# Router logits as extra columns, idle products before the gathered rows, and three roots in one batch, in a vision tower with routed experts

## The chip, the cores and the metric

One core of a Trainium2 chip runs the kernel. The metric is the device time of one execution in microseconds, as the median of three runs. The engines are TensorE (PE, its weight loads PEld), VectorE (DVE), ScalarE (ACT), GpSimd (POOL) and SyncE (SP, which issues most transfers). Each works through its own instructions in order and waits on semaphores. TensorE's clock has two levels here, 1.2 and 2.4 GHz; the profile gives the granted clock as a share of the upper one.

## What is computed

Cut to what matters:

```python
# x: 64 images of 3 x 96 x 96, 36 patches of 768 values, 256 channels, 8 experts
z = layernorm(layernorm(patches, ln1) @ W_proj + b_proj, ln2)      # 64 x 36 x 256
h = concat(cls, z) + pos_emb                                       # 37 tokens an image
x1 = norm(h)                                                       # no gain, no offset
q, k, v = x1 @ Wq.T + bq, x1 @ Wk.T + bk, x1 @ Wv.T + bv
h = h + softmax(masked(q @ k.T / 256)) @ v                         # a token does not see itself
x2 = norm(h)
logits = x2 @ router_w + router_b                                  # 8 experts
gates, experts = top2(softmax(logits))                             # gates sum to 1
# per expert the 444 tokens with the highest gates are kept
out_e = (gelu(x2[tok] @ w1[e] + b1[e]) @ w2[e] + b2[e]) * gate     # 256 -> 1024 -> 256
out = h + layernorm(scatter_add(out_e), ln)
```

The norm without gain divides by sqrt(var + 1e-5).

## The kernel before

The 2368 tokens are cut into 22 tiles of three images, 111 rows padded to 112. Behind a head of loads the kernel runs a software pipeline over the tiles: each engine has a function `step(i, slot)`, called for i = 0 to 27 in order, of which a middle part is a hardware loop over four steps at a time (ACT and DVE 6 to 17, POOL 7 to 18, PE 9 to 20). In `step(i)` an engine works for several tiles at once, each at another stage: the order of the blocks `t = i - k` in the source is the order of the queue. In the loop the waits go against register values, and `plain` adds a semaphore increment behind them.

Followed by one tile t, the stages are these. DVE takes the statistics of the patches (`stats_x`, L1046), POOL makes their root (`scale_x`), ACT normalises (L562), TensorE transposes in step t-1 (`turn_x`, L759), ACT and DVE split the result into a high and a low part (L568, L1055). TensorE multiplies by W_proj in step t (18 products, L829) and adds the bias (L831). DVE takes the statistics of z (L1129, L1137: zstat, zmv) and z2 (L1148); POOL makes the root (`rstd` with zmv); ACT scales into the residual tile H (L619); POOL adds the position (L1548); DVE takes the statistics of h (L1198, L1200: hmv). In step t+1 POOL makes the root and the offset of x1 (`scaled` with hmv), ACT makes x1 (L609). In step t+2 TensorE transposes x1 (L819), ahead of the 18 products of that step's z; in step t+3 it makes the product with the combined query-key matrix (L779), the values (L786) and the scores (L804), and transposes the probabilities at its end (L873); in step t+4 the product with the values (L812). DVE adds it to H (L1193, g_h). Then come the statistics gmv (L1133, L1141), their root on POOL (`scaled` with gmv), x2 on ACT (L633), its transpose on TensorE (L839, step t+5), its copy on ACT (L585), the product with `rw` (L795, step t+6) and the copy of the 8 logits into LG (L614).

`rstd` is an addition of epsilon (L1480) and a power of -0.5 (L1482), both on one column; `scaled` adds a multiplication by the negative mean (L1488). POOL does this four times a step: for h, z, g and the patches of a later tile. POOL also builds tables in steps 2 to 4 (`masks_table`, `live_table`, `index_table`).

In step 0 TensorE transposes Wq and Wk (L850), in step 1 it multiplies them (L858) and makes bias products of one column (L863, L866), which ACT copies out (L622 to L625). The column ED of `wv` and `bvb` carries a bias term of the scores with the values.

Behind the pipeline comes the routing. DVE picks the two best experts for the first 16 tiles in steps 22 and 23 and their gates in step 25 (`best`, `gates`, L1108 on), and the last 6 tiles when all 22 columns of LG are there. ACT repeats the gates (L665) for TensorE to transpose (L879), and an eight-round search finds each expert's threshold (L1228 to L1238, L892). Lists of tokens are made by products of one-hot rows: a short list for expert 0 (L904), then the full one in two halves (`lists`, L911). POOL gathers expert 0's rows of x2 by the short list (L1573); TensorE transposes them in two halves (`first_gathered`, L920), before each half of the full list. Then it runs, for each expert and each of 8 blocks of the hidden width, `hidden` (L944) and `project` (L961), with a gelu (L712), a cast (L724) and a difference (L1334) between them. DVE's queue there is written out by hand: the first differences, `read_lists`, two weight differences, then the first L1334.

## Time and profile before

| | |
|---|---|
| median of 3 runs | 421.92 us (421.41 to 422.31) |
| the profiled execution | 423.82 us |
| its span, first to last instruction | 421.4 us |
| PE, PEld busy | 349.8 us (83%), 312.1 us (74%) |
| DVE busy | 316.3 us (75%) |
| ACT busy | 259.0 us (61%) |
| POOL busy | 240.4 us (57%) |
| mean granted TensorE clock | 0.909 |

```profile
## 2 busy tenths in 40 slices
PE   2689999999999999660024999999999999999940
PEld 0478889999899997450013899999999999999930
DVE  7665878788777865868888555778787878787772
ACT  3336677778777785445700478686868686868520
POOL 4156888778778876310004433248686868654574
PEclk9989999999999999955555699999999999999995
```

A slice is 10.5 us and a digit is the busy share in tenths. PEclk is the granted clock in tenths: 9 is the upper level, 5 the lower.

### The profile page before, as it was taken

Reading aid. Unit: us, or ns where it says so; the run is one execution under the profiler, and the core shown is the slowest. Engines: PE = TensorE matmul, PEld = TensorE weight load, DVE = VectorE, ACT = ScalarE, POOL = GpSimd, SP = SyncE. Lnnn points to the kernel's source line nnn. Section 1 sums busy time; section 2 is a strip of 40 time slices with the busy share of each in tenths; the row PEclk is TensorE's granted clock in tenths of the full one; section 3 lists DMA queues with packets and bytes.
Section 4 is the critical chain, followed back from the end, with each engine's and each line's share of the span. In section 5 each row is a group of like instructions: output and inputs, shape, how many; then the busy total and the mean of one; then the engine's idle time right before and its main releaser. Section 6 shows DMA issues by size and latency. Waiting matters only on the chain. (4 is left out here: it accounts for less than half of the span.)

```text
span 421.4 us, 8094 instructions
## 1 busy us (share of the span) xinstructions
PE 349.8 (83%) x2190; PEld 312.1 (74%) x2190; DVE 316.3 (75%) x868; ACT 259.0 (61%) x548; POOL 240.4 (57%) x434
## 2 busy tenths in 40 slices
PE   2689999999999999660024999999999999999940
PEld 0478889999899997450013899999999999999930
DVE  7665878788777865868888555778787878787772
ACT  3336677778777785445700478686868686868520
POOL 4156888778778876310004433248686868654574
PEclk9989999999999999955555699999999999999995
DMA  6632043544535398658703587467777777752221
GB/s 185 194 64 64 2 109 109 148 135 125 145 117 144 100 121 150 169 164 239 5 0 87 154 213 192 149 155 209 209 213 206 213 207 212 206 177 56 65 76 54
DMA packets 49278, 58.38 MB, mean 139 GB/s; under 512 B 12167, under 2 KB 38007, under 8 KB 49244
## 3 DMA queue, kind: packets, MB, share of 16 engines
q1 hardware_dynamic: 42602, 43.11, 39.4%
q0 software_dynamic: 5568, 14.09, 12.7%
q10 hardware_dynamic: 1074, 0.79, 0.6%
q8 instruction: 14, 0.23, 0.2%
q14 instruction: 20, 0.16, 0.2%
HBM read 36.74 MB, written 21.36 MB: 138 GB/s over the span
## 5 line engine op out<-in xcount | busy, mean ns | idle before, releaser
L944 PE MATMUL pz<-halves 128*128 128x448 f32 x384 | 90.4, 372 | 0.0
L961 PE MATMUL pall<-halves 128*128 128x448 f32 x384 | 89.7, 369 | 0.8 <-DVE halves L1334 0.8
L944 PEld LDWEIGHTS pz<-halves 128*128 128x128 f32 x384 | 73.7, 192 | 6.1
L961 PEld LDWEIGHTS pall<-halves 128*128 128x128 f32 x384 | 71.1, 189 | 6.8 <-DVE halves L1334 1.1
L1573 POOL DMA_INDIRECT held<-x_rows,gidx x32 | 33.8, 1057 | 65.3 <-DVE gidx L1276 41.2
L712 ACT ACTIVATE wproj<-pz,b1t 128x448 f32<-128x448 f32 x64 | 40.7, 636 | 47.1 <-PE pz L944 41.3
L1334 DVE TENSOR_TENSOR halves<-wproj,halves 128x448 fp32r<-128x448 f32 x64 | 40.2, 628 | 30.5 <-ACT halves L724 25.0
L829 PE MATMUL pall<-halves 128*112 128x256 f32 x396 | 52.5, 287 | 4.6 <-DVE halves L1055 4.6
L1482 POOL TENSOR_TENSOR rs<-rs,neghalf 112x1 f32<-112x1 f32 x88 | 50.2, 570 | 7.3
L829 PEld LDWEIGHTS pall<-halves 128*112 128x112 f32 x396 | 48.1, 177 | 5.0 <-DVE halves L1055 2.7
L1598 POOL DMA_INDIRECT out<-rows,didx x28 | 37.2, 1330 | 25.6 <-DVE rows L1382 15.9
L724 ACT CAST halves<-wproj 128x448 fp32r<-128x448 f32 x64 | 36.3, 567 | 2.0
L1581 POOL DMA_INDIRECT rows<-sums,sidx x28 | 29.3, 1047 | 7.8 <-issue 7.5
L1307 DVE TENSOR_TENSOR halves<-stage,halves 128x512 fp32r<-128x512 f32 x32 | 22.0, 687 | 7.2 <-ACT halves L656 7.2
L562 ACT ACTIVATE stage<-stage,rs 112x768 f32<-112x768 f32 x22 | 22.4, 1019 | 5.3 <-POOL rs L1488 5.3
L1046 DVE BATCH_NORM_STATS2 xstat<-stage 112x6 f32<-112x384 f32 x44 | 22.3, 549 | 3.6 <-DMA stage<-in_x 3.6
L779 PE MATMUL pall<-x1T,wq 128*128 128x112 f32 x176 | 24.2, 281 | 0.5 <-ACT x2T L585 0.4
L568 ACT CAST halves<-pz 128x672 fp32r<-128x672 f32 x22 | 15.8, 719 | 12.6 <-PE pz L759 12.6
L786 PE MATMUL pall<-wv,x1T 128*112 128x257 f32 x88 | 22.8, 380 | 0.0
L779 PEld LDWEIGHTS pall<-x1T,wq 128*128 128x128 f32 x176 | 21.3, 191 | 1.8 <-issue 0.9
L1313 DVE TENSOR_TENSOR halves<-stage,halves 128x512 fp32r<-128x512 f32 x32 | 21.9, 683 | 0.0
L1055 DVE TENSOR_TENSOR halves<-pz,halves 128x672 fp32r<-128x672 f32 x22 | 18.8, 855 | 3.4 <-ACT halves L568 2.6
(265 smaller groups left out, 716.7 us busy)
## 6 DMA issues: line engine op xcount, KB each, us to landing
stage<-in_w SPq DMA_DIRECT2D x32, 512.0 KB, 5.0
stage<-in_x SPq DMA_DIRECT2D x64, 108.0 KB
x_rows<-x SPq DMA_DIRECT2D x22, 224.0 KB, 2.8
x_rows<-held SPq DMA_DIRECT2D x22, 224.0 KB, 4.2
sums<-rows SPq DMA_DIRECT2D x7, 448.0 KB
out<-held SPq DMA_DIRECT2D x21, 111.0 KB
x_rows<-zero SPq DMA_DIRECT2D x1, 1474.9 KB
wproj<-in_w_proj ACTq DMA_DIRECT2D x1, 768.0 KB
```

The source lines that it names most:

```text
L712: nc.scalar.activation(hr[:, k % 2, :], bank(k % 2)[:, 0:SLOTS], ACT.Gelu, bias=col(b1t, u)).then_inc(u_sb, 1)
L724: nc.scalar.copy(hh[:, k % 2, :], hr[:, k % 2, :]).then_inc(h_hi, 1)
L779: m = nc.tensor.matmul(bank(3)[:, o * P:(o + 1) * P], wqk[:, c, o * 128:(o + 1) * 128], xt_[:, c, :], start=(c == 0), stop=(c == EC - 1))
L786: m = nc.tensor.matmul(bank(4)[0:P, 0:ED + 1], xt_[:, c, :], wv[:, c, :], start=(c == 0), stop=(c == EC - 1))
L829: nc.tensor.matmul(bank(2)[0:P, 0:ED], xs[:, c * P:(c + 1) * P], w[:, c, :], start=(c == k == 0), stop=False)
L944: m = nc.tensor.matmul(bank(k % 2)[:, 0:SLOTS], w[:, c, k * 128:(k + 1) * 128], xs[:, e % 2, c, :], start=(n == 0), stop=(n == 3 * EC - 1))
L961: m = nc.tensor.matmul(pall[:, 2 * (e % 2) + o, 0:SLOTS], w[:, k, o * 128:(o + 1) * 128], hs[:, k % 2, :], start=(k == 0 and n == 0), stop ...
L1334: V_.tensor_tensor(hl[:, k % 2, :], hr[:, k % 2, :], hh[:, k % 2, :].bitcast(fp32), ALU.subtract)\
L1482: G.tensor_tensor(rs[:, slot, 1:2], rs[:, slot, 0:1], neghalf[:, :], ALU.pow).then_inc(done, 1)
L1573: pool.indirect_dma_start(xg[:, e % XB_N, j, :], None, x2_rows, bass.IndirectOffsetOnAxis(ap=gidx[:, k:k + 1], axis=0)).then_inc(g_in[e % ...
L1581: pool.indirect_dma_start(prev[:, j, :], None, sums[0:1 + e * SLOTS, :], bass.IndirectOffsetOnAxis(ap=sidx[:, k:k + 1], axis=0)).then_inc( ...
L1598: pool.indirect_dma_start(out, bass.IndirectOffsetOnAxis(ap=didx[0:n, k:k + 1], axis=0), final_of(e)[0:n, j, :], None, bounds_check=IMAGES ...
```

## The change

Three edits.

First, the logits. x2 @ rw is 1/sqrt(var_g + eps) times the centred h, after attention, times rw. With `rwc`, the router weights less their mean over the channels, the centring falls away, so the kernel carries (h @ rwc) as 8 more columns through the attention. `wv` and `bvb` get 8 columns Wv.T @ rwc (they pass through the probabilities with the values) and 8 columns rwc, whose product with x1, times `dev` = (var_h + eps)/sqrt(var_h + eps), is the residual's part; ACT writes it into the 8 columns behind each tile of H, which is now 264 wide. DVE's addition of L1193 adds both. ACT scales the 8 columns into LG. The transpose, copy and product of x2 and their semaphores are gone.

Second, the roots of z (tile i), h (tile i-1) and g (tile i-4) are made by one addition and one power over up to three neighbouring columns, behind one wait for all three statistics; `nrm` is double-buffered by step.

Third, 24 products of the identity by itself stand ahead of the first gathered rows.

```diff
-        wv = sb("wv", [128, EC, ED + 1])
+        HW = ED + E
+        VW = HW + 1 + E
+        wv = sb("wv", [128, EC, VW])
+        rwc = wv[:, :, HW + 1:VW]
@@ scalar, step @@
-                t = i - 5
-                if live(t):
-                    need(act, x2T_ps, t + 1)
-                    need(act, l_ps, t)
-                    nc.scalar.copy(x2T[:, :], bank(3)[:, 256:256 + EC * P]).then_inc(x2T_sb, 1)
@@ i == 0 @@
+                    act.wait_ge(c_vT, 1)
+                    nc.scalar.copy(wvs[:, :, :], bank(5)[:, 0:EC * ED].rearrange("p (c e) -> p c e", c=EC)).then_inc(c_ws, 1)
+                    nc.scalar.copy(bvrep[:, :, :], bank(7)[:, 0:EC * P].rearrange("p (c r) -> p c r", c=EC)).then_inc(c_ws, 1)
...
                 t = i - 4
                 if live(t):
-                    plain(act, (x2T_ps, t - 1), (x2_out[slot], 16 * (t // 4) if isinstance(t, int) else (t - slot) * 4),
+                    plain(act, (n_rs, i + 1), (g_h, t + 1))
+                    nc.scalar.activation(LG[:, :, at(t)] if not isinstance(t, int) else LG[:, :, t:t + 1],
+                                         tile_of(H, t, ED, HW).rearrange("p (e a) -> p e a", a=1), ACT.Copy,
+                                         scale=norm(par, 1, 2)).then_inc(l_sb, 1)
...
+                t = i - 2
+                if live(t):
+                    plain(act, (h_dev, t + 1), (v_sb, t + 1))
+                    nc.scalar.activation(tile_of(H, t, ED, HW), v[:, par, HW + 1:VW], ACT.Copy, scale=dev[:, odd:odd + 1])\
+                        .then_inc(h_rw, 1)
@@ tensor, step @@
-                        m = nc.tensor.matmul(bank(4)[0:P, 0:ED + 1], xt_[:, c, :], wv[:, c, :],
+                        m = nc.tensor.matmul(bank(4)[0:P, 0:VW], xt_[:, c, :], wv[:, c, :],
                                              start=(c == 0), stop=(c == EC - 1))
-                t = i - 6
-                if live(t):
-                    need(pe, x2T_sb, t + 1)
-                    need(pe, l_sb, t)
-                    need(pe, z_2, i if not isinstance(i, int) else min(i, TILES))
-                    for c in range(EC):
-                        m = nc.tensor.matmul(bank(2)[0:P, 256:256 + E], x2T[:, c * P:(c + 1) * P], rw[:, c, :],
-                                             start=(c == 0), stop=(c == EC - 1))
-                    m.then_inc(l_ps, 1)
...
-                    nc.tensor.matmul(bank(7)[0:P, 0:ED], probT[:, :], v[:, par, 0:ED], start=True, stop=True)\
+                    nc.tensor.matmul(bank(7)[0:P, 0:HW], probT[:, :], v[:, par, 0:HW], start=True, stop=True)\
...
-                        m = nc.tensor.transpose(bank(3)[:, 256 + c * P:256 + (c + 1) * P],
-                                                x2[:, (slot + 3) % 4, c * 128:(c + 1) * 128], ident[0:P, 0:P])
-                    m.then_inc(x2T_ps, 1)
@@ i == 0 @@
+                    for o in range(EC):
+                        for c in range(EC):
+                            nc.tensor.transpose(bank(5)[:, o * ED + c * 128:o * ED + (c + 1) * 128],
+                                                wv[:, c, o * 128:(o + 1) * 128], ident[:, :])
+                    for c in range(EC):
+                        nc.tensor.transpose(bank(7)[:, c * P:(c + 1) * P], bvb[:, c * 128:(c + 1) * 128], ident[0:P, 0:P])
+                    pe.wait_ge(c_idx, 2)
+                    for c in range(EC):
+                        m = nc.tensor.matmul(bank(6)[:, 0:E], onesf[:, :], rw[:, c, :], start=(c == 0), stop=(c == EC - 1))
+                    m.then_inc(c_vT, 1)
@@ i == 1 @@
+                    pe.wait_ge(c_ws, 4)
+                    pe.wait_ge(c_rw, 1)
+                    for c in range(EC):
+                        for o in range(EC):
+                            nc.tensor.matmul(bank(4)[:, 3 * EC + c * E:3 * EC + (c + 1) * E],
+                                             wvs[:, o, c * 128:(c + 1) * 128], rwc[:, o, :],
+                                             start=(o == 0), stop=(o == EC - 1))
+                    for o in range(EC):
+                        m = nc.tensor.matmul(bank(4)[0:P, 3 * EC + EC * E:3 * EC + EC * E + E], bvrep[:, o, :], rwc[:, o, :],
+                                             start=(o == 0), stop=(o == EC - 1))
@@ ahead of the first gathered rows @@
+            def keep_clock(n):
+
+                for _ in range(n):
+                    nc.tensor.matmul(bank(3)[:, 0:128], ident[:, :], ident[:, :], start=True, stop=True)
+            keep_clock(24)
             for h in range(2):
                 first_gathered(h)
                 lists(h)
@@ vector, step, i == 0 @@
+                    V_.memset(bvb[:, HW + 1:VW], 0.0)
+                    dve.wait_ge(c_vT, 1)
+                    V_.scalar_tensor_tensor(rwc, rep(bank(6)[:, 0:E].rearrange("p (a e) -> p a e", a=1), 1, EC),
+                                            -1.0 / ED, rw[:, :, :], ALU.mult, ALU.add).then_inc(c_rw, 1)
@@ gpsimd, step @@
-                t = i - 1
-                if live(t):
-                    need(pool, x1_ok, t)
-                    scaled(2, hmv, h_mv, t + 1, h_rs0, h_rs, h_nb)
-                t = i
-                if live(t):
-                    need(pool, z_sc, t)
-                    rstd(1, zmv, z_mv, t + 1, z_rs0, z_rs)
-                t = i - 4
-                if live(t):
-                    need(pool, x2_ok, t)
-                    scaled(3, gmv, g_mv, t + 1, g_rs0, g_rs, g_nb)
+                par = slot % 2
+                on = [k for k, back in enumerate((0, 1, 4)) if live(i - back)]
+                if on:
+                    a, b = on[0], on[-1] + 1
...
+                    plain(pool, *[((z_mv, i + 1), (h_mv, i), (g_mv, i - 3))[k] for k in on])
+                    G.tensor_scalar(nrm[:, par, 0, a:b], nmv[:, a:b, 1], EPS, None, ALU.add).then_inc(n_rs0, 1)
+                    need(pool, n_rs0, i + 1)
+                    G.tensor_tensor(nrm[:, par, 1, a:b], nrm[:, par, 0, a:b], rep(neghalf[:, :], 1, b - a), ALU.pow)\
+                        .then_inc(n_rs, 1)
+                    plain(pool, (n_rs, i + 1))
+                    for k, done in ((1, h_nb), (2, g_nb)):
+                        if k == 1 and k in on:
+                            G.tensor_tensor(dev[:, par:par + 1], norm(par, 0, 1), norm(par, 1, 1), ALU.mult).then_inc(h_dev, 1)
+                        if k in on:
+                            G.tensor_scalar(norm(par, 2, k), nmv[:, k, 0:1], norm(par, 1, k), -1.0, ALU.mult, ALU.mult)\
+                                .then_inc(done, 1)
```

`onesf` is set on POOL in the head in place of step 2, and ACT copies two more small results in step 1.

## Rows read from the trace of the kernel before

**Rows 1.** Timeline of one loop step, TensorE: start, duration, instruction, idle time before.

```profile
119.39 0.37 PE L831 MATMUL pall<-zbias,ones 2*112 2x256 f32 x1
119.68 0.41 PE L839 MATMUL pall<-ident,x 112*128 112x112 f32 x2
119.93 0.74 PE L759 MATMUL pz<-ident,stage 112*128 112x112 f32 x6
121.57 1.03 PE L786 MATMUL pall<-wv,x1T 128*112 128x257 f32 x4
122.44 0.47 PE L795 MATMUL pall<-rw,x2T 128*112 128x8 f32 x4
122.77 0.62 PE L804 MATMUL pall<-x1T,tT 128*112 128x112 f32 x4
123.66 0.35 PE L819 MATMUL pall<-ident,x 112*128 112x112 f32 x2
126.07 0.37 PE L831 MATMUL pall<-zbias,ones 2*112 2x256 f32 x1
```

**Rows 2.** The same step on the other engines, behind one earlier row.

```profile
42.91 0.26 POOL L1488 TENSOR_SCALAR rs<-hmv,rs 112x1 f32<-112x1 f32 x1
...
119.79 0.43 DVE L1129 BATCH_NORM_STATS2 zstat<-pall 112x6 f32<-112x256 f32 x1
120.73 0.18 DVE L1141 BATCH_NORM_AGGREGATE gmv<-gstat 112x2 f32<-112x6 f32 x1
122.10 0.27 POOL L1488 TENSOR_SCALAR rs<-hmv,rs 112x1 f32<-112x1 f32 x1 [0.21 <-POOL rs L1482]
122.44 0.22 POOL L1480 TENSOR_SCALAR rs<-zmv 112x1 f32<-112x1 f32 x1
122.47 0.60 ACT L609 ACTIVATE x<-held,rs 112x256 f32 x1
122.75 0.57 POOL L1482 TENSOR_TENSOR rs<-rs,neghalf 112x1 f32<-112x1 f32 x1
123.51 0.51 ACT L619 ACTIVATE held<-z,rs 112x256 f32 x1 [0.24 <-POOL rs L1482]
125.02 0.21 DVE L1051 BATCH_NORM_AGGREGATE xmv<-xstat 112x2 f32<-112x12 f32 x1
125.43 0.22 POOL L1480 TENSOR_SCALAR rs<-xmv 112x1 f32<-112x1 f32 x1
```

**Rows 3.** The power on POOL on two and on four columns: timeline, then line L1590.

```profile
408.77 0.73 POOL L1590 TENSOR_TENSOR frs<-frs,neghalf 112x2 f32<-112x2 f32 x1
...
L1590 POOL TENSOR_TENSOR frs<-frs,neghalf x9: 722/1045/1051, 271.4 to 414.7; 112x4 f32<-112x4 f32 x7, 112x2 f32<-112x2 f32 x2
```

**Rows 4.** Timeline of DVE: the statistics of z of tiles 2, 6 and 21.

```profile
34.22 0.43 DVE L1129 BATCH_NORM_STATS2 zstat<-pall 112x6 f32<-112x256 f32 x1 [3.20 <-PE pall L831]
...
59.71 0.43 DVE L1129 BATCH_NORM_STATS2 zstat<-pall 112x6 f32<-112x256 f32 x1
...
159.80 0.43 DVE L1129 BATCH_NORM_STATS2 zstat<-pall 112x6 f32<-112x256 f32 x1 [1.17 <-PE pall L831]
```

**Rows 5.** Timeline of TensorE in the head: the one-column products of step 1.

```profile
29.27 1.84 PE L863 MATMUL pall<-bqk,scratch 128*128 128x1 f32 x16
```

**Rows 6.** Timeline at the end of the pipeline: gates on DVE, repeated gates on ACT.

```profile
178.48 0.20 DVE L1108 TENSOR_SCALAR dl<-ed 112x16 f32<-112x16 f32 x1 [0.57 <-ACT ed L649]
...
183.25 1.90 ACT L665 COPY scratch<-V 112x2048 f32<-112x2048 f32 x1
```

**Rows 7.** TensorE's timeline before the experts; then 238 to 240 us by engine, with PEclk.

```profile
220.15 2.19 PE L904 MATMUL pall<-scratch 112*112 112x4 bf16 x22 [4.63 <-DVE scratch L1266]
...
234.13 4.83 PE L944 MATMUL pz<-halves 128*128 128x448 f32 x12
...
238.79 1.59 PE L961 MATMUL pall<-halves 128*128 128x448 f32 x6
...
238.00:240.00 2.00, 2.00 (x8) 1.50 (x7) 1.23 (x2) 1.48 (x3) 1.70 (x2) 0.74 0.94 306
```

More of the change, by code:

```diff
@@ L154, in vit_tower @@
         zstat = sb("zstat", [P, 6])
-        zmv = sb("zmv", [P, 2])
         z2 = sb("z2", [P, ED])
         hstat = sb("hstat", [P, 6])
-        hmv = sb("hmv", [P, 2])
         x1 = sb("x1", [P, 2, ED])
@@ L171, in vit_tower @@
         gstat = sb("gstat", [P, 6])
-        gmv = sb("gmv", [P, 2])
         x2 = sb("x2", [P, 4, ED])
-        x2T = sb("x2T", [128, EC * P])
-        rs = sb("rs", [P, 4, 3])
+        rs = sb("rs", [P, 1, 3])
+        nmv = sb("nmv", [P, 3, 2])
+        zmv, hmv, gmv = (nmv[:, k, :] for k in range(3))
+        nrm = sb("nrm", [P, 2, 3, 3])
+        dev = sb("dev", [P, 2])
         held = sb("held", [P, XB_N * JT * XW])
-        assert TILES * ED <= XB_N * JT * XW
-        H = held[:, 0:TILES * ED].rearrange("p (t f) -> p t f", t=TILES)
+        assert TILES * HW <= XB_N * JT * XW
+        H = held[:, 0:TILES * HW].rearrange("p (t f) -> p t f", t=TILES)
         xg = held[:, :].rearrange("p (s j f) -> p s j f", s=XB_N, j=JT)
@@ L489, in step @@
                     need(sp, hb, t + 1)
-                    tile = H[:, t:t + 1, :] if isinstance(t, int) else H[:, bass.ds(t, 1), :]
+                    tile = H[:, t:t + 1, 0:ED] if isinstance(t, int) else H[:, bass.ds(t, 1), 0:ED]
                     dram = hb_v[:, 2 * t:2 * t + 2, :] if isinstance(t, int) else hb_v[:, bass.ds(t * 2, 2), :]
@@ L608, in step @@
                     plain(act, (x1T_ps, t - 1), (h_nb, t + 1))
-                    nc.scalar.activation(x1[:, odd, :], tile_of(H, t), ACT.Identity, bias=rs[:, 2, 2:3],
-                                         scale=rs[:, 2, 1:2]).then_inc(x1_ok, 1)
-                t = i - 5
-                if live(t):
-                    plain(act, (l_ps, t + 1))
-                    nc.scalar.copy(LG[:, :, at(t)] if not isinstance(t, int) else LG[:, :, t:t + 1],
-                                   bank(2)[0:P, 256:256 + E].rearrange("p (e a) -> p e a", a=1)).then_inc(l_sb, 1)
+                    nc.scalar.activation(x1[:, odd, :], tile_of(H, t), ACT.Identity, bias=norm(par, 2, 1),
+                                         scale=norm(par, 1, 1)).then_inc(x1_ok, 1)
                 t = i
                 if live(t):
-                    plain(act, (z_2, t + 1), (z_rs, t + 1))
-                    nc.scalar.activation(tile_of(H, t), z2[:, :], ACT.Copy, scale=rs[:, 1, 1:2]).then_inc(z_sc, 1)
+                    plain(act, (z_2, t + 1), (n_rs, i + 1))
+                    nc.scalar.activation(tile_of(H, t), z2[:, :], ACT.Copy, scale=norm(par, 1, 0)).then_inc(z_sc, 1)
                 if isinstance(i, int) and i == 1:
@@ L825, in step @@
                     need(pe, z_2, t)
-                    need(pe, l_sb, t - 5)
                     for c in range(PC):
@@ L832, in step @@
                         .then_inc(z_ps, 1)
-                t = i - 5
-                if live(t):
-                    need(pe, x2_ok, t + 1)
-                    need(pe, x2T_sb, t)
-                    need(pe, t_sb, t + 3 if not isinstance(t, int) else min(t + 3, TILES))
-                    for c in range(EC):
-                        m = nc.tensor.transpose(bank(3)[:, 256 + c * P:256 + (c + 1) * P],
-                                                x2[:, (slot + 3) % 4, c * 128:(c + 1) * 128], ident[0:P, 0:P])
-                    m.then_inc(x2T_ps, 1)
                 t = i + 1
@@ L1135, in step @@
                 if live(t):
-                    plain(dve, (z_st, t + 1), (z_rs0, t))
-                    V_.bn_aggr(zmv[:, :], zstat[:, :]).then_inc(z_mv, 1)
+                    plain(dve, (z_st, t + 1), (n_rs0, t))
+                    V_.bn_aggr(zmv, zstat[:, :]).then_inc(z_mv, 1)
                 t = i - 4
@@ L1140, in step @@
                     plain(dve, (g_st, t + 1), (g_nb, t))
-                    V_.bn_aggr(gmv[:, :], gstat[:, :]).then_inc(g_mv, 1)
+                    V_.bn_aggr(gmv, gstat[:, :]).then_inc(g_mv, 1)
                 t = i
@@ L1163, in step @@
                     need(dve, o_ps, t - 1)
-                    V_.tensor_tensor(v[:, par, :], bank(4)[0:P, 0:ED + 1], bvb[:, :], ALU.add).then_inc(v_sb, 1)
+                    need(dve, h_rw, t - 1)
+                    V_.tensor_tensor(v[:, par, :], bank(4)[0:P, 0:VW], bvb[:, :], ALU.add).then_inc(v_sb, 1)
                     plain(dve, (s_ps, t + 1), (p_ok, t), (s_nmx, t))
@@ L1191, in step @@
                 if live(t):
-                    need(dve, r_inv, t + 1)
-                    V_.scalar_tensor_tensor(tile_of(H, t), bank(7)[0:P, 0:ED], rinv[:, 0:1], tile_of(H, t),
+                    plain(dve, (r_inv, t + 1), (h_rw, t + 1))
+                    V_.scalar_tensor_tensor(tile_of(H, t, 0, HW), bank(7)[0:P, 0:HW], rinv[:, 0:1], tile_of(H, t, 0, HW),
                                             ALU.mult, ALU.add).then_inc(g_h, 1)
```

80 lines of the change are left out of this document (45 added, 35 removed).

## The prediction

> **What bounds the kernel now.** I read the page first: TensorE is 83% busy and, in its slices, at nine tenths and full clock in two stretches, the token and attention loop (to about 170 us) and the experts (from about 240 us to the end), with the router's search between them at the lower clock. The change touches the loop, the search's entry and the experts' first products.
>
> In the loop I read the timeline of one step. TensorE has no idle mark in it: from one bias product L831 to the next are 6.68 us, and everything else has its answer early enough [rows 1]. The 15 steps between the statistics at 59.71 and 159.80 take 6.67 us each [rows 4]. So a TensorE product taken out saves its own time, until some other chain of one step is as long. I therefore looked for such a chain in the new program before adding up savings.
>
> **Router logits out of TensorE's stream.** Gone per step: two transposes of x2 (L839, 119.68 to 119.93: 0.25 us) and the logits products (L795, 122.44 to 122.77: 0.33 us) [rows 1]. Added: 16 columns in the value products and 8 in the residual product. L786 with 257 columns takes 0.87 us for two products (121.57 to 122.44) [rows 1], so 0.43 us for one; 16 more in each of two and 8 more in one are 0.07 us. Net 0.51 us: were TensorE still the limit, a step would be 6.16 us.
>
> **The roots as one batch: a new ring.** Before, x1's root belongs to tile i-1 and is made first on POOL; ACT starts x1 at 122.47 and TensorE wants its transpose L819 at 123.66 [rows 1, 2]. Now POOL's one addition waits for zmv of tile i too. ACT's x1 of tile i-1 thus hangs on z of tile i, and TensorE transposes that x1 ahead of z of tile i+1, in order. This is a chain that must be walked once a step:
> - L831 to zstat 0.40 (119.39 to 119.79); zstat to the end of gmv 1.12 (120.91) [rows 1, 2].
> - to POOL 0.20 (xmv ends 125.23, L1480 at 125.43); addition and gap 0.31 (122.44 to 122.75) [rows 2].
> - the power. One column takes 0.57 [rows 2], two 0.73, four 1.045 [rows 3]: 0.16 a column, so three columns 0.885, an estimate between two measured widths.
> - gap 0.21 (the mark at L1488) [rows 2]; dev, a product that the trace does not show: not below L1480's 0.22, not above the power's 0.57; it is one arithmetic step on one column, so I take 0.22; gap 0.08; the scale 0.27.
> - to ACT 0.19 (the power ends 123.32, ACT starts 123.51), x1 0.60 [rows 2]; to TensorE 0.10, an estimate: no row shows TensorE waiting for x1 here, the nearest handover is POOL's at 122.37 to ACT's start at 122.47 [rows 2].
> - L819 to L831 2.41 (123.66 to 126.07) [rows 1].
> Sum 7.00 us, against 6.67 now: TensorE idles 0.84 us a step and the step is 0.33 us longer. For the 12 steps that ACT and DVE run as a loop (6 to 17) +3.9 us. In the last three (18 to 20) the waits are constants and shorter: L1488 at 42.91, outside the loop, has no idle mark where the loop's has 0.21 [rows 2]. Four such handovers at 0.1 less make about 6.6 us: -0.3 us. Bounds of the ring: with the power at two columns' 0.73 and TensorE next at once 6.75 (+0.9 us in 12 steps); with power 1.045 and dev 0.57 7.51 (+10 us).
>
> The GPSIMD Engine Reference of the Trainium skill (Elementwise, side-by-side cycle accounting) puts the price in a per-instruction part and about 2.6 cycles per element. By that, two more columns cost nothing one could see, which is rival B. The trace disagrees for the power, at 0.16 us a column [rows 3], and the sum goes by the trace.
>
> POOL itself gets freer: two power instructions of 0.57 us and two additions less a step. That gives nothing, since POOL's tile additions wait for ACT's z. The queue behind the batch on POOL (position, x scaling, ln_b) ends about 0.8 us before the next gmv. On ACT the x2T copy goes and the small h_rw copy comes, at the step's end, where ACT then waits for TensorE; the wider DVE additions (8 and 16 columns) lie in DVE's waits; together 0, at most 0.1 us a step if they reached the ring. SP's queue is the same.
>
> **The head (steps 0 to 5).** Step 0's new transposes, the ones product, two ACT copies and rwc on DVE lie in waits that step 0 has for its tiles anyway; nothing, up to 0.5 us. Step 1's six small products (12 instructions) lie on the path, between the q-k products and z of tile 2. At L863's rate (1.84 us for 16) [rows 5] they are 1.4 us, at L795's (0.33 for four [rows 1]) 1.0; I take 1.2 us. From step 2 on the ring holds too. Now 34.22 to 59.71 is 25.49 us for four steps [rows 4]. With constant waits the ring is about 6.1 us with two live norms (steps 2, 3) and 6.55 with three (4, 5), and POOL's tables behind step 2 delay the next batch by a further 1.2 us, as they do partly now. Sum 26.5 us, with the tables' smaller delays 26.7: +1.2 us. The head is +2.5 us (1.2 to 4), less where the extra products keep the clock up early.
>
> **The drain.** LG of the last tile was copied only after x2, transpose, copy and product; L665 stands right behind it on ACT, at 183.25 [rows 6]. Now it needs statistics, root and one scaled copy. Counted from the last zstat (159.80 [rows 4]) with the durations of the step above [rows 2]: x1 of tile 20 ends at 3.7; POOL adds the position to tile 21 by 5.0, its statistics are there at 5.7 and the next batch (two columns, in DVE's order behind g's statistics) gives x1 of tile 21 at 8.9; its values, scores and exponentials, with DVE's two top-2 pieces between them, put the residual sums of tiles 20 and 21 at 14.5 and 18.0. That is about 0.8 us later than now; gates of the first 16 tiles (L1108 at 178.48, 18.7 us behind zstat [rows 6]) move to 19.4 behind it and end at 21.65; LG of tile 21 is there by 20.1. So L665 and the second top-2 start 21.75 us behind the last zstat in place of 23.45: -1.8 us (-1 to -3). What is late next is the gates, not the logits.
>
> **24 idle products.** They start at the end of the short list, 222.34 [rows 7], when the granted clock is 0.50 (1.2 GHz). Each is fp32 on 128 columns, about 0.43 to 0.45 us at the low clock, 0.22 to 0.24 at the full one (half of L786's 257 columns). The experts' products started 234.13 and the clock rose within 238 to 240 (mean 0.74) [rows 7], some 4.9 us behind them. A like delay gives 11 products low and 13 fast, so they end at 230.1 and the first gathered rows, which now are taken at 227.3, wait 2.8 us. Then four transposes, half the list, four transposes and half the list at full clock end at 233.3, hidden(0,0) starts 233.6 in place of 234.13 and takes 1.25 in place of 2.4 us. Its gelu, cast and difference, and DVE's list reading and two weight differences in front of that, put project(0,0) at 237.2 in place of L961's 238.79 [rows 7]. With that product itself at full clock: -1.6 us. Bounds: the rise 1.5 us sooner, -2.2; clock fallen again before the experts, -0.4; no rise, all 24 slow (to 233), +3.
>
> **Sum.** +2.5 + 3.9 - 0.3 - 1.8 - 1.6 = +2.7 us. The experts behind are unchanged. The profiled execution had a span of 421.4 us and took 423.82, 1.9 above the median of 421.92; its span would be 424.1, and the median 424.6 us.
>
> **Rivals.**
> A: TensorE stays the bound (x1 does not come late). Then 16 steps of -0.51 are -8, head +1, drain -2, products -1.6: 411 us. For it: POOL and ACT both have free time. Against it: the five waits in a row above; it would need them to sum to under 6.2 us.
> B: the power of three columns costs one column's 0.57, or the handovers are as much shorter: ring 6.69 us, loop +0.2 and head +1.5, so drain and products win: 421.92 + 1.7 - 0.3 - 1.8 - 1.6 = 419.9 us. For it: the handovers were read in steps in which TensorE was the limit. Against it: three widths on one line [rows 3].
> C, slower by more: the power and dev at the upper bounds, 7.3 us or more a step from step 4 on, decided when power and dev sum to over 1.4 us: 429 us. Against it: only 0.885 lies on the line through three widths.
> D: the idle products cost: the clock does not rise while they run and they end at 233, past the second pair of gathered rows: +3 in place of -1.6, 429 us.
>
> Forecast 0.54, A 0.07, B 0.18, C 0.13, D 0.08. About 0.2% (0.84 us) can be told from no change. Slower: forecast 0.46, C, D: 0.67; within: the forecast's edge and a part of B 0.12; faster: A and the rest of B 0.21. The forecast's own range is 422.3 to 427; the whole one, 419.5 to 429, leaves out A and the far end of C.
>
> **What would show it.** zstat to zstat in the middle of the loop at 6.9 to 7.1 us; an idle mark of TensorE before x1's transpose put down to ACT x1, and one of ACT before x1 put down to POOL; the power on 112x3 at 0.88 us; the clock full from about 227 us; ACT's keys copy 21.7 us behind the last zstat. It is wrong if TensorE shows no idle time in the loop, or the power takes about 0.6 us.

## The result: 425.54 us, and the profile after

The changed kernel takes 425.54 us (median of 5 runs, 424.62 to 427.54) against 421.95 (421.41 to 422.31): a ratio of 1.0075, 95% interval 1.0053 to 1.0097. Forecast: 424.6. The profiled execution took 427.54 us with a span of 425.7, 4.3 above the span of before. The change's four other executions took 424.62 to 425.59 us.

One step of the loop, TensorE, in the changed kernel (start, duration, instruction, idle time before and who ended it), the answer to [rows 1]:

```profile
119.08 0.37 PE L835 MATMUL pall<-zbias,ones 2*112 2x256 f32 x1
...
121.00 1.09 PE L800 MATMUL pall<-wv,x1T 128*112 128x273 f32 x4
...
123.84 0.41 PE L824 MATMUL pall<-ident,x 112*128 112x112 f32 x2 [0.91 <-ACT x L616]
...
126.31 0.37 PE L835 MATMUL pall<-zbias,ones 2*112 2x256 f32 x1
```

Before there was no idle mark in this step. Now there is one, 0.91 us, and ACT's x1 ended it. All 12 loop steps have this mark, 0.55 to 0.91 us, 8.3 us together; before, TensorE has no idle mark in any of them. The chain in front of it in the same step, DVE, POOL and ACT [rows 2]:

```profile
119.57 0.43 DVE L1150 BATCH_NORM_STATS2 zstat<-pall 112x6 f32<-112x256 f32 x1 [0.57 <-PE pall L835]
120.57 0.18 DVE L1162 BATCH_NORM_AGGREGATE nmv<-gstat 112x2 f32<-112x6 f32 x1
121.06 0.24 POOL L1562 TENSOR_SCALAR nrm<-nmv 112x3 f32<-112x3 f32 x1 [0.86 <-DVE nmv L1162]
121.38 0.88 POOL L1564 TENSOR_TENSOR nrm<-nrm,neghalf 112x3 f32<-112x3 f32 x1
122.45 0.19 POOL L1569 TENSOR_TENSOR dev<-nrm 112x1 f32<-112x1 f32 x1 [0.18 <-POOL nrm L1564]
122.73 0.50 POOL L1571 TENSOR_SCALAR nrm<-nmv,nrm 112x1 f32<-112x1 f32 x2
123.19 0.60 ACT L616 ACTIVATE x<-held,nrm 112x256 f32 x1 [1.40 <-POOL nrm L1571]
```

Read from top to bottom, this is one chain: each row waits for the work of the one above, or stands behind it in the same engine's queue (as the statistics of g behind those of z, and x1's offset behind `dev`). The step shown took 7.14 us from zstat to zstat; the loop's four slots differ, and the next three took 6.87, 7.02 and 6.99. Over the whole run the profile's waits say the same (line, what it waited for, us in total, times, longest):

```profile
POOL nrm L1562 <- DVE nmv L1162: 21.8, 20, 3.6
PEld pall L824 <- ACT x L616: 21.5, 21, 1.6
...
ACT x L616 <- POOL nrm L1571: 13.8, 13, 1.7
```

The statistics of z of tiles 2, 6, 18 and 21 [rows 4]:

```profile
36.40 0.43 DVE L1150 BATCH_NORM_STATS2 zstat<-pall 112x6 f32<-112x256 f32 x1 [4.80 <-PE pall L835]
...
63.41 0.43 DVE L1150 BATCH_NORM_STATS2 zstat<-pall 112x6 f32<-112x256 f32 x1 [0.77 <-PE pall L835]
...
147.59 0.43 DVE L1150 BATCH_NORM_STATS2 zstat<-pall 112x6 f32<-112x256 f32 x1 [0.48 <-PE pall L835]
...
167.79 0.43 DVE L1150 BATCH_NORM_STATS2 zstat<-pall 112x6 f32<-112x256 f32 x1 [1.01 <-PE pall L835]
```

(147.59 - 63.41) / 12 = 7.015 us a step; before it was 6.672 (59.71 to 139.77).

The head on TensorE [rows 5], with the new small products (L877, L881), and the granted clock in two stretches (PEclk is the last column but two):

```profile
30.74 1.04 PE L877 MATMUL pall<-wv,scratch 128*128 128x8 f32 x8
31.63 0.54 PE L881 MATMUL pall<-wv,scratch 128*112 128x8 f32 x4
32.02 0.43 PE L824 MATMUL pall<-ident,x 112*128 112x112 f32 x2
32.19 3.88 PE L833 MATMUL pall<-halves 128*112 128x256 f32 x18
```

```profile
15.00:20.00 5.00, 4.16 (x19) 3.94 (x19) 2.21 (x5) 1.03 (x1) 1.07 (x3) 0.52 0.66 201
...
32.00:36.00 4.00, 4.00 (x23) 3.85 (x22) 0.00 (x0) 2.07 (x8) 1.05 (x3) 0.57 0.18 55
```

The end of the pipeline [rows 6]:

```profile
186.49 0.19 DVE L1129 TENSOR_SCALAR dl<-ed 112x16 f32<-112x16 f32 x1 [0.55 <-ACT ed L663]
187.34 0.31 ACT L637 ACTIVATE LG<-held,nrm 112x8 f32<-112x8 f32 x1 [0.88 <-POOL nrm L1564]
187.74 1.53 POOL L1589 TENSOR_TENSOR held<-held,lnb 112x256 f32<-112x256 f32 x2
187.96 0.70 DVE L1141 TENSOR_TENSOR V<-V 112x128 f32<-112x128 f32 x1
188.58 0.75 DVE L1112 TENSOR_TENSOR LG<-LG,rbb 112x48 f32<-112x48 f32 x1
188.69 1.90 ACT L679 COPY scratch<-V 112x2048 f32<-112x2048 f32 x1 [0.23 <-DVE V L1141]
```

And TensorE before the experts [rows 7]:

```profile
226.24 2.18 PE L919 MATMUL pall<-scratch 112*112 112x4 bf16 x22 [4.63 <-DVE scratch L1292]
228.28 8.15 PE L926 MATMUL pall<-ident 128*128 128x128 f32 x48
...
239.66 2.74 PE L964 MATMUL pz<-halves 128*128 128x448 f32 x12
243.24 1.45 PE L981 MATMUL pall<-halves 128*128 128x448 f32 x6 [0.84 <-DVE halves L1360]
```

The difference by stage, from the two profiled executions (us, after less before):

| stage | measured | forecast |
|---|---|---|
| head, to the statistics of z of tile 6 | +3.70 | +2.5 |
| 12 loop steps, tile 6 to 18 | +4.12 | +3.9 |
| steps 18 to 20, tile 18 to 21 | +0.17 | -0.3 |
| drain, tile 21's zstat to ACT's keys copy | -2.55 | -1.8 |
| search, keys copy to the short list | +0.65 | 0 |
| idle products, short list to project(0,0) | -1.64 | -1.6 |
| experts, to the last project | -0.32 | 0 |
| sum (last project at 407.85, before 403.72) | +4.13 | +2.7 |

### The profile page after: what moved, and what is told of

Read it like the earlier page. It is cut to its first block, busy times and chain, and to the rows that moved or that the text cites. A ratio compares the mean times of both kernels' runs of the same rounds, so it can differ in the third digit from the quotient of the medians.

```text
span 425.7 us, 7910 instructions
## 1 busy us (share of the span) xinstructions
PE 346.9 (81%) x2128; PEld 303.9 (71%) x2128; DVE 320.6 (75%) x870; ACT 255.8 (60%) x552; POOL 220.9 (52%) x376
## 4 chain that ended last, share of the span: by engine, by line
PE 61%; DVE 14%; issue 11%; POOL 8%; ACT 4%; DMA 1%; POOLq 0%; DVEq 0%; ACTq 0%
PE pall L981 18%; PE pz L964 18%; PE pall L833 11%; POOL nrm L1564 4%; ACT x L616 3%; DVE wproj L1254 2%; PE pall L926 2%; PE pall L824 2%; PE pall L992 2%; PE pall L835 1%; POOL nrm L1562 1%; PE pall L950 1%; PE pall L765 1%; POOL nrm L1571 1%; DVE gstat L1154 1%
## 5 line engine op out<-in xcount | busy, mean ns | idle before, releaser
L964 PE MATMUL pz<-halves 128*128 128x448 f32 x384 | 88.2, 366 | 0.1
L964 PEld LDWEIGHTS pz<-halves 128*128 128x128 f32 x384 | 72.0, 188 | 6.0 <-DVE halves L1371 0.2
L833 PE MATMUL pall<-halves 128*112 128x256 f32 x396 | 55.1, 296 | 2.2 <-DVE halves L1076 2.2
L833 PEld LDWEIGHTS pall<-halves 128*112 128x112 f32 x396 | 50.7, 186 | 2.4 <-DVE zbias L1095 2.4
L1578 POOL TENSOR_TENSOR held<-held,posb 112x256 f32 (+1 forms) x22 | 16.2, 737 | 24.3 <-ACT held L621 22.5
L616 ACT ACTIVATE x<-held,nrm 112x256 f32 (+1 forms) x22 | 13.2, 600 | 24.0 <-POOL nrm L1571 13.8
L1333 DVE TENSOR_TENSOR halves<-stage,halves 128x512 fp32r<-128x512 f32 x32 | 22.0, 687 | 7.1 <-ACT halves L670 7.1
L800 PE MATMUL pall<-wv,x1T 128*112 128x273 f32 x88 | 23.9, 394 | 0.0
L1150 DVE BATCH_NORM_STATS2 zstat<-pall 112x6 f32<-112x256 f32 x22 | 9.4, 429 | 17.6 <-PE pall L835 17.6
L1564 POOL TENSOR_TENSOR nrm<-nrm,neghalf 112x3 f32<-112x3 f32 (+2 forms) x26 | 21.1, 810 | 2.3 <-POOL nrm L1562 0.2
```

The lines of the kernel that those rows point to most:

```text
L616: nc.scalar.activation(x1[:, odd, :], tile_of(H, t), ACT.Identity, bias=norm(par, 2, 1), scale=norm(par, 1, 1)).then_inc(x1_ok, 1)
L800: m = nc.tensor.matmul(bank(4)[0:P, 0:VW], xt_[:, c, :], wv[:, c, :], start=(c == 0), stop=(c == EC - 1))
L833: nc.tensor.matmul(bank(2)[0:P, 0:ED], xs[:, c * P:(c + 1) * P], w[:, c, :], start=(c == k == 0), stop=False)
L964: m = nc.tensor.matmul(bank(k % 2)[:, 0:SLOTS], w[:, c, k * 128:(k + 1) * 128], xs[:, e % 2, c, :], start=(n == 0), stop=(n == 3 * EC - 1))
L1564: G.tensor_tensor(nrm[:, par, 1, a:b], nrm[:, par, 0, a:b], rep(neghalf[:, :], 1, b - a), ALU.pow)\
```

## Experiments

Ratios are to the kernel before, measured beside each experiment on the same chip; the changed kernel's own is 1.0075. The edits are shortened to what matters. "Step" is (zstat of tile 18 less zstat of tile 6) / 12 in the run's profile: 6.67 before, 7.015 in the change.

**e1: the change with three separate roots.**

```diff
-  G.tensor_scalar(nrm[:, par, 0, a:b], nmv[:, a:b, 1], EPS, ...)      # one addition, one power
-  G.tensor_tensor(nrm[:, par, 1, a:b], nrm[:, par, 0, a:b], rep(neghalf, 1, b - a), ALU.pow)
+  # h, then z, then g: each with its own wait, addition and power on one column
```

> The changed kernel with its second edit undone: the roots of h, z and g are made one after the other again, each as its own addition and power on one column; logits columns and idle products stay. Theory (the batch closes a chain z, statistics, power, x1, transpose, z of 7.0 us a step): x1 leaves the chain, TensorE's idle mark before x1's transpose goes. But POOL then has as much work as before plus dev; before, it went from one step's first addition to the next with gaps of 0.1 us only, so I expect POOL to set the step at 6.85 to 6.95 us, and the median at 423.5 to 425 us. Rival (TensorE is the only limit once the chain is open): 6.2 us a step, about 412 us. Rival (the chain was not what held the step): 7.0 us still, 425.5 us.

Measured 422.08 us against 423.08, ratio 0.9979 (0.9959 to 0.9999), step 6.79. Without the batch the rest of the change costs nothing, but the 0.51 us taken from TensorE don't arrive: the step is even 0.12 longer than before. POOL goes round without a wait longer than 0.21 us. One step of POOL is 6.83 us here, from position to position:

```profile
101.03 0.74 POOL L1580 TENSOR_TENSOR held<-held,posb 112x256 f32 x1
...
102.93 0.26 POOL L1511 TENSOR_SCALAR rs<-xmv,rs 112x1 f32<-112x1 f32 x1 [0.21 <-POOL rs L1509]
...
107.86 0.74 POOL L1580 TENSOR_TENSOR held<-held,posb 112x256 f32 x1
```

So POOL's queue now sets the step, and `dev` lengthens it. The expectation of the step (6.85 to 6.95) was 0.06 too high at its lower edge, that of the median (423.5 to 425) 1.4 us. It also expected TensorE's idle mark before x1's transpose to go. It shrank instead: 10 of the 12 loop steps still have it, 4.2 us together for the change's 8.3. The mark no longer tells of the ring: the root of h has no wait before it on POOL (L1554, without an idle mark in all 12 steps), so x1 is late because POOL's queue is.

```profile
120.03 0.41 PE L824 MATMUL pall<-ident,x 112*128 112x112 f32 x2 [0.55 <-ACT x L616]
```

**e2: h's root ahead and alone, z and g as a pair.**

```diff
-  on = [k for k, back in enumerate((0, 1, 4)) if live(i - back)]      # z, h, g in one batch
+  # h: addition, power, dev, offset; does not wait for z of this step
+  on = [k for k, back in enumerate((0, 4)) if live(i - back)]         # then z and g
```

> The changed kernel with the root of h made alone and first, on one column, and z and g as a batch of two columns behind it. Theory: the chain through x1 is open and POOL has one power instruction less than with three roots apart (about 6.35 us of work a step), so the step is 6.3 to 6.45 us and the median 414 to 417 us. Rival (the handovers, not the order, cost the time): 6.9 to 7.0 us a step, 425 us.

Measured 419.00 against 423.08, ratio 0.9902 (0.9885 to 0.9920), step 6.69. The step was expected at 6.3 to 6.45 us and the median at 414 to 417: both promised too much gain. The ring is gone: in no loop step does the root of h wait on POOL for a statistic. TensorE still waits for x1 in 8 of the 12 loop steps, 3.0 us together, because POOL's round is long. POOL waits inside it: 0.41 us for ACT's scaled z before the position, 0.26 for ACT's x scaling after it, with the ln_b addition queued behind both.

```profile
105.23 0.74 POOL L1581 TENSOR_TENSOR held<-held,posb 112x256 f32 x1 [0.41 <-ACT held L621]
```

**e5: e2, and the ln_b addition ahead of the position.**

```diff
+  t = i - 5: need(pool, x2_ok, t + 1); tile_of(H, t) += lnb           # before the position
   t = i: tile_of(H, t) += posb
   ...
-  t = i - 5: need(pool, x2_ok, t + 1); tile_of(H, t) += lnb           # at the step's end
```

> The kernel with h's root alone and z and g as a pair, in which POOL's addition of ln_b (0.73 us) is moved ahead of its addition of the position. The pair alone gave 6.69 us a step, not 6.35, because POOL stood idle between the pair and the position while ACT scaled z (0.9 us with both handovers). Theory: the ln_b addition fills that wait, POOL's round falls to about 6.0 us and TensorE's 6.16 sets the step: 6.15 to 6.3 us, and the median 4 to 6 us under that of the pair alone, 0.976 to 0.981 of the kernel before. Rival (another engine's queue, DVE's or ACT's, holds the step): 6.5 us or more, less than 3 us gained.

Measured 412.81 against 422.08, ratio 0.9779 (0.9747 to 0.9812), step 6.20. That is faster than both kernels. The addition fills the place of the wait, POOL goes round in 6.1 us, and TensorE is the limit with the step that the prediction gave it if nothing else were (6.16):

```profile
119.72 0.27 POOL L1575 TENSOR_SCALAR nrm<-nmv,nrm 112x1 f32<-112x1 f32 x1 [0.21 <-POOL nrm L1571]
119.94 0.73 POOL L1581 TENSOR_TENSOR held<-held,lnb 112x256 f32 x1
120.63 0.74 POOL L1587 TENSOR_TENSOR held<-held,posb 112x256 f32 x1
```

**e9: the whole change, only the ln_b addition moved**, as in e5.

> The whole change, with POOL's addition of ln_b moved from the end of its step to just behind the batch of three roots. This order took 0.5 us a step out of the loop when h's root had a batch of its own. Theory (in the change as it stands the chain zstat, three statistics, batch, x1, transpose is the bound, and POOL waits 0.6 to 0.9 us a step for gmv): POOL's order gives nothing, 6.9 to 7.0 us from zstat to zstat, ratio to the change 0.998 to 1.002, so 1.006 to 1.010 of the kernel before. Rival (POOL's queue is the bound in the change too, its wait only a symptom): 6.5 us a step, ratio 0.99 of the kernel before.

Measured 426.71 against 421.85, ratio 1.012 (1.0087 to 1.0154), step 7.014. The step is the change's to 0.001 us. POOL's wait for gmv grows from 0.60 to 0.86 us (two steps of the change) to 1.29 to 1.55 (two steps of e9): the queue isn't the bound there, the ring is. The total is 0.002 above the band that I gave; the intervals of the two ratios overlap.

**e12 and e10: POOL's side alone, on the kernel before.** e12 takes the batches of e5 without touching the logits; e10 moves the ln_b addition alone.

```diff
-  rstd(1, zmv, ...); scaled(3, gmv, ...)
+  G.tensor_scalar(nrm[:, par, 0, 0:2], nmv[:, 0:2, 1], EPS, ...)      # z and g, e12 only
+  G.tensor_tensor(nrm[:, par, 1, 0:2], nrm[:, par, 0, 0:2], rep(neghalf, 1, 2), ALU.pow)
+  t = i - 5: ... += lnb                                               # before the position, both
```

> The kernel before with POOL's side alone: h's root stays a batch of its own, z and g share one addition and one power, ln_b is added ahead of the position. The logits stay in TensorE's stream, and there are no idle products. POOL's queue gets shorter by an addition and a power, 0.22 + 0.57 - 0.14 = 0.6 us a step, TensorE's stays. Theory (two queues stood at 6.67 us a step, so relief of one gives nothing: the logits alone gave 6.79, this gives 6.67, and both together gave 6.20): zstat to zstat 6.65 to 6.70 us, ratio 0.997 to 1.003. Rival (POOL was the only bound and TensorE was just kept full by it): 6.2 to 6.5 us a step, ratio 0.985 to 0.995.

> The kernel before, with the same move of the ln_b addition. Theory: there POOL goes round in 6.67 us (5.9 busy and four gaps of 0.21 behind a power), exactly TensorE's step, without any wait on another engine of more than 0.24; moving an addition leaves POOL's sum as it is and TensorE at its limit, so 6.67 us a step and a ratio of 1.000 (0.997 to 1.003). Rival (the order matters by itself: the patches' root comes 0.73 us later and delays the next tile's stage): slower, 1.005 to 1.01.

e12: 423.75 against 422.38, ratio 1.0031 (1.0014 to 1.0047), step 6.665. e10: 422.02 against 421.85, 1.0013 (0.9996 to 1.0030), step 6.63. In e12 POOL waits 0.83 us for DVE's statistics and TensorE's step is what it was:

```profile
119.22 0.22 POOL L1485 TENSOR_SCALAR rs<-xmv 112x1 f32<-112x1 f32 x1 [0.83 <-DVE xmv L1056]
```

With e1 and e5 this makes a square: logits alone 6.79, POOL alone 6.67, both 6.20 us a step. Neither edit gives anything without the other. (e1 also has `dev` on POOL; the logits without `dev` were not run.) e12's ratio is at the edge of what was expected; the last section has a likely part of it.

One reading in e10's expectation is wrong: in the kernel before, POOL does wait for another engine by more than 0.24 us. 9 of the 12 loop steps have a wait for DVE's statistics of the patches, 2.5 us together, the longest 0.46:

```profile
118.90 0.22 POOL L1480 TENSOR_SCALAR rs<-xmv 112x1 f32<-112x1 f32 x1 [0.46 <-DVE xmv L1051]
```

That is 0.2 us a step. TensorE, with no idle mark in the same 12 steps, was the limit before, and POOL's own round stood some 0.2 us below it, at 6.46 us. Adding `dev` and its gap (0.28) gives an estimate of 6.74 us for e1, which measured 6.79.

**e4: the batch widened to five columns.** The two more columns are read by nobody.

```diff
+  if b - a == 3:
+      b = 5
```

> The changed kernel with the batch of three roots widened to five columns, two of them constants that nobody reads: one suspected cost increased. Theory (the power costs 0.16 us a column and lies on the chain): the power takes 1.20 us, the step 7.32 us, and about 16 steps give 430.5 us (429.5 to 431.5). Rival (a power instruction costs by the instruction, and the handovers made the step long): the power 0.9 us, 425.6 us.

Measured 435.91 against 423.08, ratio 1.0294 (1.0272 to 1.0317), step 7.33. The power takes 1.20 us, and the step grows by the same 0.32: what POOL's power costs is paid in full. The total is higher than the 429.5 to 431.5 us expected. About 16 steps were counted, so the 12 of the loop and four more. Against the change, the profile has +1.99 us to tile 6, +0.95 from tile 18 to 21 and a drain longer by 1.84 (22.74 for 20.90), and the experts, which the edit doesn't touch, took 1.28 us longer (last section).

```profile
125.90 1.20 POOL L1567 TENSOR_TENSOR nrm<-nrm,neghalf 112x5 f32<-112x5 f32 x1
```

**e8: `dev` behind the two offsets**, off the way to x1.

```diff
-  if k == 1 and k in on: G.tensor_tensor(dev[...], norm(par, 0, 1), norm(par, 1, 1), ALU.mult)   # before the offset
+  if 1 in on: G.tensor_tensor(dev[...], norm(par, 0, 1), norm(par, 1, 1), ALU.mult)              # behind both
```

> The changed kernel with dev computed behind the two scales in place of ahead of them; the same instructions, one order. Theory (dev lies on the chain ahead of x1's offset): the step falls by dev and its gap, 0.28 us, to 6.73, and the median by 4 to 5 us against the changed kernel, to 1.000 of the kernel before (0.997 to 1.003). Rival (POOL's total work holds the step): no change, 1.0085.

Measured 423.21 against 422.08, ratio 1.0018 (0.9997 to 1.0039), step 6.75. One small product off the ring takes 0.26 us from each step. TensorE still waits for x1 in all 12 loop steps, 5.2 us together for the change's 8.3. By the ratios the whole is 2.4 us faster than the change, where 4 to 5 were expected.

**e7: the batch of three alone, on the kernel before.**

```diff
-  scaled(2, hmv, ...); rstd(1, zmv, ...); scaled(3, gmv, ...)
+  # the change's batch, without dev; logits and their products as before, no idle products
```

> The kernel before with the batch of three roots alone (no dev, logits by TensorE as before, no idle products). Theory: the chain is the one of the changed kernel without dev, 7.00 - 0.28 = 6.72 us, next to TensorE's own 6.67: the step stays within 0.1 us of before, and head and drain cost 0.5 to 1.5 us by their longer powers: 0.5 to 2 us slower than before, ratio 1.001 to 1.005. Rival (the batch frees POOL and lets the step shrink): faster than before.

Measured 426.05 against 422.08, ratio 1.0091 (1.0067 to 1.0115), step 6.77. More than expected. The step is 0.10 above before and 0.14 above e10, which has the same clock pattern in the head; that is 1.2 to 1.7 us in 12 steps. TensorE has only two idle marks there, 0.4 us together, so it and the ring are about equally long, as the theory has it; what makes the rest of the 0.10 was not found. Up to project(0,0) e7's profile stands 1.75 behind that of e10, and at the last project 2.97: another 1.2 us come in the experts, which the edit doesn't touch (below).

**e6, e3: the idle products alone, and the change without them.**

```diff
+  keep_clock(24)          # e6: the kernel before with this line
-  keep_clock(24)          # e3: the change without it
```

> The kernel before with the 24 idle products alone. Theory (worth 1.6 us): ratio 0.9962, about 1.6 us faster than before; from the short list's start to the first product of the second layer 17.0 us in place of 18.64. Rival (they delay the gathered rows as much as they save): 1.000.

> The changed kernel without the 24 idle products. Theory (they bring the full clock to the first experts' products for a wait of the gathered rows, worth 1.6 us): 427.1 us, 1.2 to 2.2 above the changed kernel; the first product of the second layer comes 1.6 us later behind the short list. Rival (the later gathered rows take the gain back): 425.5 us or less.

e6: 420.32 against 422.08, 0.9952 (0.9933 to 0.9971); from the short list to project(0,0) 17.38 us in its profile, where 17.0 was expected and 18.64 stood before. e3: 428.56 against 423.08, 1.0132 (1.0112 to 1.0152). Added to before they give 0.5%; taken out of the change they cost 0.6%. In e3's profile the short list starts as in the change (226.26 and 226.24), and project(0,0) at 244.89 in place of 243.24: 1.65 us.

**e11: e5 with 12 idle products.**

```diff
-  keep_clock(24)
+  keep_clock(12)
```

> The best version so far (h's root ahead and alone, ln_b addition ahead of the position, ratio 0.978), with 12 idle products in place of 24. There the 24 take 8.1 us, and the clock reaches the full level some 5 us into them. Theory (work between the products' end and the experts keeps the clock, and the rows have long been gathered): 12 products take 5.2 us, the experts start 1.5 to 2.5 us sooner at full clock: ratio 0.972 to 0.976. Rival (12 are not enough, the clock rises only within the experts' first products, as without any): the experts start about 1 us sooner but their first twelve products take 4.3 in place of 2.6 us, and the halves of the list 2.2 in place of 1.3: ratio 0.978 to 0.983.

Measured 415.49 against 421.85, ratio 0.9859 (0.9824 to 0.9894): worse than 24 (0.9779), and a little worse than even the rival had it. TensorE then waits for the gathered rows, twice, and the clock falls back before the experts:

```profile
220.32 0.42 PE L940 MATMUL pall<-ident,held 112*128 112x112 f32 x2 [0.62 <-DMA held<-x_rows,gidx]
...
223.90 0.64 PE L940 MATMUL pz<-ident,held 112*128 112x112 f32 x2 [1.78 <-DMA held<-x_rows,gidx]
...
226.36 4.30 PE L964 MATMUL pz<-halves 128*128 128x448 f32 x12
```

```profile
220.00:224.00 4.00, 1.91 (x27) 1.70 (x28) 2.58 (x4) 0.53 (x1) 0.90 (x1) 0.89 0.44 119
224.00:228.00 4.00, 4.00 (x28) 3.83 (x29) 2.52 (x10) 0.53 (x1) 0.93 (x1) 0.50 0.00 0
```

The expected time of the 12 products was 5.2 us, and they took 5.5. From the short list to project(0,0) it takes 19.2 us (211.81 to 231.03), in e5 17.0 (210.41 to 227.37). The other 1.4 us between the two profiles lie ahead of it, in the head, where e11's clock was low twice (0.50 in 15 to 20, 0.58 in 32 to 36). I had the rows "long gathered", since with 24 products no wait is seen; in fact the first half's last rows came 8.5 us behind the short list's start, and the 24 products of e5 end at 10.0. Most of their time covers a wait that is there anyway.

## Why the prediction was right, and where its terms were off

**The ring: right, in mechanism and size.** Forecast 7.00 us a step, measured 7.015. All the marks named are there: TensorE's before x1's transpose, ACT's before x1, the power on three columns at 0.88 (0.885 forecast). `dev` was priced at 0.22 and took 0.19. The sum is better than its terms. Over the 12 loop steps the means are: L835 to zstat 0.43 us (0.40 forecast), gmv to POOL 0.27 (0.20), the gap behind the power 0.17 (0.21), the offset with its handover to ACT 0.40 (0.46), x1 to the transpose 0.05 (0.10), L824 to L835 2.47 (2.41). Misses up and down cancel; in the longest of the four slots, shown above, the whole chain adds up to 7.23. TensorE idles 0.69 us a step, where 0.84 was forecast. e4 and e8 lengthen and shorten the ring by one instruction each, and the step follows: +0.32 and -0.26. Rival A needed no ring and rival B a power without a price per column; e4 and the profile exclude both. Rival B is what the GPSIMD Engine Reference of the Trainium skill gives (Elementwise, side-by-side cycle accounting), about 2.6 cycles per element, which the page measured on an addition. For the power the trace differs: one, two, three, four and five columns take 0.57, 0.72, 0.88, 1.045 and 1.20 us, 0.16 us each.

**The head: the mechanism right, the term +2.5 measured +3.7.** The products of step 1 (L877 from 30.74 until x1's transpose at 32.02) take 1.28 us of TensorE, forecast 1.2. The rest of the miss is the clock: in this profile it was at the lower level in 32 to 36 (mean 0.57), behind a stretch in which TensorE was busy all the time and at the full level, and z of tile 2 took 3.88 us for 18 products where the same 18 take 2.35 in the loop. That is 1.5 us in this one execution. e9 and e10, the change and the kernel before but for the same moved addition, both had the low stretch early (15 to 20 us at 0.66) and none at 32 to 36. Their statistics of z of tile 6 are at 61.34 and 58.91: +2.43, against +2.5 forecast. e6 has the unchanged head of the kernel before and the same early low stretch: 58.58, which makes it +2.76, of which 1.25 stand at tile 2 already (34.35 and 33.10) and 1.51 come up to tile 6 (1.2 forecast). So the head's own cost is 2.4 to 2.8 us, and the comparison of the two profiled executions has 0.9 to 1.3 us of clock on top. The medians hardly have this part: the change's four other executions had a mean granted clock of 0.926, like e9's profiled one, where the profiled one of the change had 0.919.

**Steps 18 to 20: the wrong sign, 0.5 us.** I compared the ring with constant waits (6.6) with 6.67. The three steps take 6.73 each (147.59 to 167.79): the first still 6.89, the others 6.66 and 6.65. So two of them are as long as before, and the one at the loop's edge isn't.

**The drain: -2.55 for -1.8.** The forecast's own figures, 21.75 in place of 23.45, make -1.7. The gates are late next, as said, and not the logits: ACT's keys copy waits for V of the first 16 tiles. They ended 20.9 behind the last zstat and not 21.65; the gates' block began at 186.49, 18.7 behind zstat as before, so the 0.7 us that I let them slip did not happen.

**A term that I did not have: +0.65 in the search's entry.** The second top-2 now starts when V is done, and meets POOL's ln_b additions, which before had ended by then. Its first addition takes 0.75 us (188.58 to 189.33) where it took 0.21, and ends with POOL's, at 189.27. The row has 0.75 or 0.76 us in all nine kernels with the change's logits (the change, e1 to e5, e8, e9, e11), where POOL adds twice at that time, and 0.21 in the five others, where it doesn't. Of the 0.65 us, which count from ACT's keys copy, this makes 0.29, since the top-2 starts 0.26 sooner against that copy than before. The other 0.36 come in one round of the search, in which DVE waits 0.65 us for TensorE's product where the same round had 0.29 before; the cause was not found:

```profile
204.96 0.16 DVE L1264 SCALAR_TENSOR_TENSOR cand<-pz,rest 128x1 int32<-128x1 int32 x1 [0.65 <-PE pz L907]
```

For the slow addition the GPSIMD Engine Reference of the Trainium skill (Specifications) has a rule: GpSimd's SBUF interfaces are shared with VectorE, with contention for VectorE instructions with two SBUF inputs. The trace agrees, with an addition longer by 0.54 us; that it is this mechanism, no run tests.

**The idle products: right.** -1.64 for -1.6. The products end at 236.4, 8.15 us behind their start, where 7.8 was forecast; the clock is at the lower level up to 233 and at the full one from 234 on. e6 and e3 show a gain without and with the rest of the change, by the medians; in the profiles it is 1.26 us in e6 (18.64 less 17.38) and 1.63 against e3.

**The sum** was +2.7, the medians differ by 3.6 and the spans by 4.3. The sign and the place were right. Of the 0.9 us between the forecast of the medians' difference and the measured one, the smaller misses make +0.3 (+0.2 loop, +0.5 steps 18 to 20, +0.65 search, -0.75 drain, -0.3 experts), and the head's own up to +0.3 more. The rest isn't found, and the single executions of each kernel differ by as much. That misses of up to 0.75 us cancel is luck; the large terms are not.

**What the prediction did not see** is how close POOL stood to the limit. It says that POOL "gets freer" and that this "gives nothing". In the change as it stands that holds (e9). But POOL's round before was 6.46 us without its waits for DVE, 0.2 below TensorE's step. So, by this estimate, not more than 0.2 of the 0.51 us taken from TensorE could have arrived, even without a ring, and `dev` took that back (e1). The profile hides this: POOL is 57% busy on the page because that is a mean over stages, and in the loop its gaps of 0.21 us behind a power don't look like a queue. The batch gave POOL what the logits gave TensorE, and took it back by tying h's root to z of the next tile. The same savings with h untied, and the ln_b addition in the place of a wait, are worth 2.2% (e5).

## What to carry to other kernels

Before crediting a saving on the busiest engine, lay out one step of every other engine and add its gaps that a dependence on itself makes: where that sum comes close to the step, the second queue takes over after a small part of the saving. A batch over several tiles joins their waits; the member that is wanted first should stay out of it, if another waits for work of the same step. Idle products to raise the clock are cheapest where TensorE would wait for a transfer anyway, and here 12 were worse than 24.

## What the hardware showed that I had not expected

The clock in the head has no fixed place. The profiled execution of the kernel before had its low stretch at 24 to 27.4 us, others had theirs in 15 to 20 alone (e5, e6, e9, e10), and the changed kernel had two, at 15 to 22 and at 32 to 36. e5 and e11 are the same program up to the idle products: with one low stretch e5 has its statistics of z of tile 6 at 60.37, with two e11 has them at 61.87. So a second stretch makes some 1.5 us, and a head is compared between executions with the same pattern.

The experts' products ran at one of two paces at a granted clock of 1.00 throughout. The median product on 448 columns took 365 ns in most profiled executions (366 in e9 and e11) and 368 in those of e4, e7 and e12; line L948 of e7 in 260 to 380 us (duration minimum, median, maximum):

```profile
L948 PE MATMUL pz<-halves x270: 362/368/369, 260.8 to 380.0; 128*128 128x448 f32 x135
```

From project(0,0) to the last one e10 takes 164.95 us, e7 166.17 and e12 165.97, so 1.0 to 1.2 us more; e4 takes 165.89 for the change's 164.61. Against e10, e7's last project is 2.97 us later, 1.75 of them from the loop and the rest from here; e12's is 2.56 later, of which 1.15 come in the head, where its clock was low twice. Whether the slower pace belongs to these programs or to these executions stays open. The chip alone doesn't decide it: e7 ran on the chip of e5, e6 and e8, and e4 on that of e1 to e3, which have 365.
